# Choosing two experts batch by batch inside attention, with the gates computed beside the counting

## The reference

```python
logits = jnp.einsum('bsh,eh->bse', x, gate_w) + expert_bias
weights = jax.nn.softmax(logits, axis=-1)
top_w, top_i = jax.lax.top_k(weights, K)            # K = 2
top_w = top_w / (jnp.sum(top_w, axis=-1, keepdims=True) + GATE_EPS)
...                                                  # 8 experts, each token's two weighted and summed
out = (out - mu) * jax.lax.rsqrt(var + LN_EPS)
return out + x                                       # x here is the second layer norm's output
```

## Time and profile before

| | |
|---|---|
| three runs | 1274.6, 1275.29, 1277.65 us; median 1275.29 |
| the profiled execution | 1278.43 us, of which its span (first to last instruction) is 1276.7 us |
| busy share of the span | PE 87%, DVE 61%, POOL 65%, ACT 50% |
| attention, first to last `add_bias` | 77.7 to 715.0 us |
| tail of attention, from there to the first instruction of route | to 742.2 us |
| route | 742.2 to 793.6 us |
| experts | from 793.6 us |

### The profile page before, as it was taken

The page is one execution under the profiler, slowest core; times in us unless marked ns, Lnnn a source line. Parts: engine busy times, 40 slices in busy tenths (PEclk is TensorE's granted clock), DMA queues, the critical chain, the costliest instruction groups (busy, mean ns, idle before and its releaser), DMA issues. The chain is left out here.

```text
span 1276.7 us, 30578 instructions
## 1 busy us (share of the span) xinstructions
PE 1105.3 (87%) x11290; PEld 882.5 (69%) x11291; DVE 783.3 (61%) x2073; ACT 633.4 (50%) x904; POOL 832.1 (65%) x925
## 2 busy tenths in 40 slices
PE   5559999999999999999999717999999999999900
PEld 3237777777777777777777613888888888888800
DVE  4626668567576675766868566555555555555567
ACT  3438786776767777777777400222222222222222
POOL 2337587687776887768857521566766666666656
PEclk9769999999999999999999955999999999999955
DMA  8985854863558537565273182242434344432364
GB/s 281 289 213 130 245 146 115 202 142 99 139 141 190 140 100 161 141 139 170 61 180 101 69 281 66 39 113 48 115 49 108 47 111 112 90 74 45 45 163 135
DMA packets 122892, 167.14 MB, mean 131 GB/s; under 512 B 13048, under 2 KB 99320, under 8 KB 122784
## 3 DMA queue, kind: packets, MB, share of 16 engines
q1 hardware_dynamic: 103200, 137.59, 39.7%
q0 software_dynamic: 19584, 28.11, 11.9%
HBM read 105.22 MB, written 60.44 MB: 130 GB/s over the span
## 5 line engine op out<-in xcount | busy, mean ns | idle before, releaser
L983 DVE CUSTOM_DVE_ANT_0 b_sn<-b_ps_s,s_tile 128x512 f32<-128x512 f32 x512 | 341.5, 689 | 194.6 <-PE b_ps_s L1136 191.5
L920 ACT ACTIVATE b_pt<-b_ps_t 128x1024 f32<-128x1024 f32 x256 | 259.2, 1016 | 74.2 <-PE b_ps_t L1150 74.2
L1150 PE MATMUL b_ps_t<-ident,b_sn 128*128 128x128 f32 x2048 | 268.6, 274 | 3.1 <-POOL b_sn L820 2.0
L1150 PEld LDWEIGHTS b_ps_t<-ident,b_sn 128*128 128x128 f32 x2048 | 237.4, 141 | 41.0 <-issue 10.7
L1758 ACT ACTIVATE d_g<-d_ps_u 128x512 f32<-128x512 f32 x156 | 92.8, 598 | 305.8 <-PE d_ps_u L1871 216.5
L820 POOL TENSOR_SCALAR b_sn<-b_sn,b_mn 128x512 f32<-128x512 f32 x256 | 175.9, 698 | 97.8 <-DVE b_mn L983 97.4
L912 ACT ACTIVATE b_sn<-b_sn,b_mn 128x512 f32<-128x512 f32 x256 | 182.2, 723 | 94.6 <-DVE b_mn L983 87.5
L1136 PE MATMUL b_ps_s<-s_ks,s_qs 96*128 96x512 bf16 x512 | 179.2, 386 | 30.0 <-PEq L145 19.7
L1871 PE MATMUL d_ps_u<-d_xp,k_wu 128*128 128x256 bf16 x1776 | 201.5, 274 | 0.1
L1886 PE MATMUL d_ps_y<-k_wd,d_gp 128*128 128x256 bf16 x1776 | 199.9, 273 | 0.0
L1871 PEld LDWEIGHTS d_ps_u<-d_xp,k_wu 128*128 128x128 bf16 x1776 | 173.4, 98 | 21.9 <-issue 0.9
(11 more groups left out here) (237 smaller groups left out, 1171.4 us busy)
## 6 DMA issues: line engine op xcount, KB each, us to landing
w_parts<-b_w_split SPq DMA_DIRECT2D x32, 512.0 KB, 3.6
splits<-s_parts SPq DMA_DIRECT2D x32, 384.0 KB, 3.2
s_qs<-splits SPq DMA_DIRECT2D x96, 128.0 KB, 5.9
s_ks<-splits SPq DMA_DIRECT2D x96, 128.0 KB, 7.5
b_w_raw<-in_w_up_t SPq DMA_DIRECT2D x16, 512.0 KB, 11.1
b_w_raw<-in_w_down_t SPq DMA_DIRECT2D x16, 512.0 KB, 7.4
k_wu<-w_parts SPq DMA_DIRECT2D x8, 1024.0 KB
k_wd<-w_parts SPq DMA_DIRECT2D x8, 1024.0 KB
```

Of the source, the lines that this page charges most:

```text
L920: act.activation(pt[:, m, 2 * pair:2 * pair + 2, :], ps_t[:, 2 * pair:2 * pair + 2, :], ACT.Exp).then_inc(exped, 1)
L983: dve.tensor_tensor_reduce(sn[:, n % 2, t, :], ps_s[:, t % 2, :], ahead.tile[:, n, at:at + S], -1.0, BIG, ALU.add, ALU.min, mn[:, n % 2, t ...
L1150: mm = pe.transpose(ps_t[:, j, t * P:(t + 1) * P], sn[:, m, t, j * P:(j + 1) * P], ident[:, :])
```

## The change

1. `logits`, `top`, `top_i` and the two tiles that held the last rows (`xb`, `gated`) move into a class `Choice` that lives from attention to the end.
2. `keep_logits` adds the expert bias while it copies. The searches run on these biased logits and not on the softmax weights (the order is the same). For batch b - 2 they stand in batch b: four `max` at n = 1.5, two `max_index` at n = 2.5, two at n = 3.5. Batch 6's stand at the end of the last batch's heads, batch 7's behind the last logits.
3. In route the chain from the bias to the gates is gone from the DVE's beginning. After `both`, two subtractions (l - l1 for all eight, l2 - l1) are issued, ACT takes exp of both, and behind `kept.rows` the gates follow as 1 / (1 + e + eps * sum) and e times that.
4. In the tail of attention, the second half of the last rest moves from POOL to the DVE (two instructions, between the last copy for the logits and the logits). SP issues the last store of rest and no longer waits for it or for the rows there: route's SP waits ahead of the load of rest, route's POOL ahead of the first gathers.

```diff
@@ new class @@
+class Choice:
...
+        self.logits = sb("logits", [P, NT, NE])
+        self.e_bias = sb("e_bias", [P, NE])
+        self.top = sb("top", [P, NT, 8])
+        self.top_i = sb("top_i", [P, NT, 8], U32)
+        self.rows, self.rest = sb("rows", [P, TB, D]), sb("rest", [P, TB, D])
+        self.rows_out, self.rest_out = (ctx.enter_context(nc.semaphore("h_rows_out")),
+                                        ctx.enter_context(nc.semaphore("h_rest_out")))
@@ attention, SP @@
             by_batches(batch)
             store_h2(B - 1)
-            store_rest(B - 1)
-            sp.wait_ge(h2_out, 16 * B)
-            sp.wait_ge(rest_out, 16 * B)
+            sp.wait_ge(dve_end, by_dve("rest"))
+            sp.wait_ge(rest_done, B * 2 - 1)
+            sp.dma_start(rest_rows[B - 1, :, :].rearrange("(t p) d -> p t d", p=P), gated[:, :, :]).then_inc(rest_out, 16)
             sp.wait_ge(sums_zeroed, 16 * (B + 1))
             sp.wait_ge(w_stored, 16 * 4 * NE)
@@ attention, POOL @@
             deviation(B - 1)
-            for j in range(2):
-                rest_of(B - 1, j)
+            rest_of(B - 1, 0)
@@ attention, DVE @@
             def keep_logits(b, at):
                 dve.wait_ge(used, at + 1)
-                dve.tensor_copy(logits[:, bass.ds(b * TB, TB), :],
-                                ps_m[:, 0:TB * NE].rearrange("p (t e) -> p t e", e=NE)).then_inc(freed, 1)
+                dve.tensor_tensor(logits[:, b * TB:(b + 1) * TB, :], ps_m[:, 0:TB * NE].rearrange("p (t e) -> p t e", e=NE),
+                                  ahead.e_bias[:, :].unsqueeze(1).to_broadcast([P, TB, NE]), ALU.add).then_inc(freed, 1)
+
+            def largest(b):
+
+                for t in range(b * TB, (b + 1) * TB):
+                    dve.max(top[:, t, :], logits[:, t, :]).then_inc(topped, 1)
+
+            def largest_at(b, ts):
+
+                dve.wait_ge(topped, (b + 1) * TB)
+                apart(dve, dve_passed)
+                for t in ts:
+                    dve.max_index(top_i[:, b * TB + t, :], top[:, b * TB + t, :], logits[:, b * TB + t, :])
...
+                if b > 1:
+                    if n == 1.5:
+                        dve.wait_ge(freed, use(b - 1, "middle", "logits") + 1)
+                        apart(dve, dve_passed)
+                        largest(b - 2)
+                    if n == 2.5:
+                        largest_at(b - 2, (0, 1))
+                    if n == 3.5:
+                        largest_at(b - 2, (2, 3))
...
             by_batches(batch)
+            dve.wait_ge(freed, ALL_USES)
+            largest(B - 2)
+            largest_at(B - 2, range(TB))
             dve.wait_ge(pe_end, by_pe("turn0"))
...
+            mod = mod_last[:, 2 * D:3 * D].unsqueeze(1).to_broadcast([P, 2, D])
+            by_gate = ot[:, :].rearrange("p (t d) -> p t d", d=D)
+            dve.tensor_tensor(by_gate, xb[:, 2:4, :], mod, ALU.mult).then_inc(dve_end, 1)
+            dve.wait_ge(dve_end, by_dve("scaled"))
+            dve.tensor_tensor(gated[:, 2:4, :], gated[:, 2:4, :], by_gate, ALU.add).then_inc(dve_end, 1)
             dve.wait_ge(pe_end, by_pe("logits"))
-            dve.tensor_copy(logits[:, (B - 1) * TB:, :], ps_m[:, 0:TB * NE].rearrange("p (t e) -> p t e", e=NE))
+            dve.tensor_tensor(logits[:, (B - 1) * TB:, :], ps_m[:, 0:TB * NE].rearrange("p (t e) -> p t e", e=NE),
+                              ahead.e_bias[:, :].unsqueeze(1).to_broadcast([P, TB, NE]), ALU.add).then_inc(dve_end, 1)
+            dve.wait_ge(dve_end, by_dve("logits"))
+            largest(B - 1)
+            largest_at(B - 1, range(TB))
@@ route, SP @@
+            sp.wait_ge(choice.rest_out, 16 * B)
             sp.dma_start(kept.rest[:, :, :], rest_rows.rearrange("b (t p) d -> p (b t) d", p=P)).then_inc(kept_in, 16)
@@ route, POOL @@
             pool.wait_ge(tokens_set, 1)
+            pool.wait_ge(choice.rows_out, 16 * B)
@@ route, ACT @@
-            act.wait_ge(shifted, 1)
-            act.activation(weights[:, :, :], logits[:, :, :], ACT.Exp).then_inc(exped, 1)
+            act.wait_ge(shifted, 2)
+            act.activation(weights[:, :, :], weights[:, :, :], ACT.Exp).then_inc(exped, 1)
+            act.activation(per_tok[:, 1, :], per_tok[:, 0, :], ACT.Exp).then_inc(exped, 1)
@@ route, DVE @@
-            link(dve.tensor_tensor(logits[:, :, :], logits[:, :, :], e_bias[:, :].unsqueeze(1).to_broadcast([P, NT, NE]), ALU.add))
-            link(dve.tensor_reduce(per_tok[:, 0, :], logits[:, :, :], AX.X, ALU.max))
...
-            for t in range(NT):
-                ins = dve.max(top[:, t, :], weights[:, t, :])
-            link(ins)
-            for t in range(NT):
-                ins = dve.max_index(top_i[:, t, :], top[:, t, :], weights[:, t, :])
-            link(ins)
-            link(dve.tensor_tensor(per_tok[:, 3, :], top[:, :, 0], top[:, :, 1], ALU.add))
...
             link(dve.tensor_copy(top_f[:, :, :], top_i[:, :, 0:2]))
             dve.wait_ge(consts_ready, 9)
...
             dve.tensor_tensor(both[:, :, :], hot[:, 0, :, :], hot[:, 1, :, :], ALU.add).then_inc(hot_done, 1)
+
+
+            dve.tensor_tensor(weights[:, :, :], logits[:, :, :], top[:, :, 0:1].to_broadcast([P, NT, NE]), ALU.subtract).then_inc(shifted, 1)
+            dve.tensor_tensor(per_tok[:, 0, :], top[:, :, 1], top[:, :, 0], ALU.subtract).then_inc(shifted, 1)
 
             dve.wait_ge(ranked, 1)
...
             link(dve.tensor_copy(kept.rows[:, :, :], places[:, :, :]))
+            dve.wait_ge(exped, 2)
+            link(dve.tensor_reduce(per_tok[:, 2, :], weights[:, :, :], AX.X, ALU.add))
+            link(dve.scalar_tensor_tensor(out=per_tok[:, 2, :], in0=per_tok[:, 2, :], scalar=GATE_EPS, in1=per_tok[:, 1, :],
+                                          op0=ALU.mult, op1=ALU.add))
+            link(dve.tensor_scalar(per_tok[:, 2, :], per_tok[:, 2, :], 1.0, None, ALU.add))
+            link(dve.reciprocal(per_tok[:, 3, :], per_tok[:, 2, :]))
+            dve.tensor_copy(kept.gates[:, 0, :], per_tok[:, 3, :]).then_inc(gates_set, 1)
+            dve.tensor_tensor(kept.gates[:, 1, :], per_tok[:, 3, :], per_tok[:, 1, :], ALU.mult).then_inc(gates_set, 1)
             rows = kept.rows[:, :, :].rearrange("p k t -> p (k t)")
```

More of the change, by code:

```diff
@@ L56, in make_identity, with __init__, sb @@
                        pattern=[[-1, P]], channel_multiplier=1).then_inc(done, 1)
+class Choice:
+    def __init__(self, nc, ctx):
+        def sb(name, shape, dt=F32):
+            return ctx.enter_context(nc.sbuf_tensor("h_" + name, shape, dt))
+        self.logits = sb("logits", [P, NT, NE])
[5 more added lines that the diff above has]
+                                        ctx.enter_context(nc.semaphore("h_rest_out")))
 class Ahead:
@@ L498, with attention @@
 FROM_BEFORE = ("back3", "turn0", "turn1", "out0", "out1", "rows0", "rows1", "logits")
-def attention(nc, ahead, logits, x, h1t, mod_rows, ext_rows, splits, w_up_t, w_down_t, w_parts, rest_rows, h2_rows, sums):
+def attention(nc, ahead, choice, x, h1t, mod_rows, ext_rows, splits, w_up_t, w_down_t, w_parts, rest_rows, h2_rows, sums):
     GROUPS = NH // TB
@@ L528, in attention @@
         ont = sb("ont", [P, DC, S])
-        xb = sb("xb", [P, TB, D])
+        logits, top, top_i, xb, gated = choice.logits, choice.top, choice.top_i, choice.rows, choice.rest
         ga = sb("ga", [P, D])
         gab = sb("gab", [P, D])
-        gated = sb("gated", [P, TB, D])
         mod2 = sb("mod2", [P, 3 * D])
@@ L583, in attention @@
                    "rows00", "rows01", "rows10", "rows11", "logits")
-        DVE_ENDS = ("ont0", "on", "ont1b", "rows0", "rows1")
+        DVE_ENDS = ("ont0", "on", "ont1b", "rows0", "rows1", "scaled", "rest", "logits")
         def by_pe(name):
@@ L1350, in __init__, with route @@
         self.wd = sb("wd", [P, 2, PIECES, NIC, D], BF16)
-def route(nc, kept, logits, rest_rows, mod_rows, e_bias, w_parts, gate_rows, h2_rows):
+def route(nc, kept, choice, rest_rows, mod_rows, w_parts, gate_rows, h2_rows):
     FILLS = TABLE * TT
@@ L1477, in _ @@
             link(dve.memset(swing[:, 1:NE:2], -1.0))
-            link(dve.tensor_tensor(logits[:, :, :], logits[:, :, :], e_bias[:, :].unsqueeze(1).to_broadcast([P, NT, NE]), ALU.add))
-            link(dve.tensor_reduce(per_tok[:, 0, :], logits[:, :, :], AX.X, ALU.max))
-            dve.tensor_tensor(logits[:, :, :], logits[:, :, :], per_tok[:, 0, :].unsqueeze(2).to_broadcast([P, NT, NE]),
-                              ALU.subtract).then_inc(shifted, 1)
-            dve.wait_ge(exped, 1)
-            link(dve.tensor_reduce(per_tok[:, 1, :], weights[:, :, :], AX.X, ALU.add))
-            link(dve.reciprocal(per_tok[:, 2, :], per_tok[:, 1, :]))
-            link(dve.tensor_tensor(weights[:, :, :], weights[:, :, :], per_tok[:, 2, :].unsqueeze(2).to_broadcast([P, NT, NE]), ALU.mult))
-            for t in range(NT):
-                ins = dve.max(top[:, t, :], weights[:, t, :])
-            link(ins)
-            for t in range(NT):
```

(7 more changed lines are left out.)

20 lines of the change are left out of this document (9 added, 11 removed).

## The result

The changed kernel took a median of 1266.07 us over five runs (1263.28 to 1269.97), the kernel before 1274.6 over five runs (1271.43 to 1277.65), the three from which the forecast started among them. The ratio is 0.9945, 95% interval 0.9924 to 0.9966: faster by 4.3 to 9.7 us, and the forecast of 7.6 lies inside. The median of 1266.07 lies inside the stated 1264.5 to 1271.5.

A forecast was written before the change was run, and what follows sets the result against it. One serial stretch from attention's end through route to experts, in which steps hang mostly on the DVE, was taken as the bound. 3.1 + 6.1 - 0 - 1.55 - 0 = 7.6 us less than 1275.29 gives 1267.7; range 1264.5 to 1271.5.

The forecast's parts named there:

- The end of attention: From the last logits to route's start: without POOL's second half and SP's wait, route starts 3.1 us earlier (2.9 to 3.25).
- The tail: DVE work behind the last logits: bias and copy, four maxima, four index searches, together 1.26 us.
- the meeting point: Between attention's last engine and route's start: taken as 0.35 us, between bounds of 0.2 and 0.5.
- Rest on the DVE: Two added DVE passes before the last logits, 0.69 to 1.33 us each, hidden behind PE's logits.
- The start of route: DVE chain to `hot`, 11.43 us before: now POOL's constants are late, `hot` comes after 5.35, gain 6.1 us.
- The subtractions: Between `both` and the ranks in route: 0.42 and 0.21 us fit the DVE's idle 0.70, cost 0 (0 to 0.1).
- The gates: In route, between `kept.rows` and the places' bits: on the path in full, a loss of 1.55 us (1.4 to 1.9).
- The slots: Searches in attention's batches 2 to 7: hidden where the DVE waits for PE, cost 0; without cover 6.2 us.
- The first: Rival at attention's end: the store is waited for all the same, gain 5.9 us, time 1269.4; chance 0.12.
- second: Rival in attention: the searches there are on the path, 6.2 of 7.6 us go, time 1273.9; chance 0.06.
- third: Rival in attention: index searches cost far more there, at 2 us per slot the time is 1284; chance 0.02.
- The fourth: Rival in route's token search: PE returns to full clock, 5 us more gain, time 1263; chance 0.04.

## Why the prediction was right

**The end of attention** was worth 3.05 against 3.1, by two errors of opposite sign. The tail took 1.39 and not 1.26 (the maxima start 0.04 behind the copy's end, but the first index search only 0.15 behind the maxima's), and the meeting point 0.26 and not 0.35. That the sum fits to 0.05 is partly luck. The two bounds, 0.2 and 0.5, belonged to different last engines. The DVE's drain here ends at 731.4, 0.04 behind its last search, and route begins 0.2 behind it; with POOL computing both halves route begins 0.2 behind SP's drain too, but that drain stands 0.3 behind the end of SP's issue. So the 0.35 lay between two cases and belonged to neither.

**Rest on the DVE.** The two passes took 2.35 us together, from 727.03 to 729.38, within 1.38 and 2.66, and 0.61 of PE's logits remained as cover. The split differs from what was worked out: the DVE's first pass began 0.05 ahead of POOL's addition and took its plain 0.68; POOL's took 1.75 instead of 1.27; the DVE's second pass took 1.64 and ended 0.55 behind POOL's end at 728.83, so it too got hardly anything done until then. The Trainium skill (SBUF — State Buffer, Who interferes with whom) has whoever issues second wait for the whole of the first; the trace agrees to within 0.15, with the DVE first this time: by the rule POOL would end at 727.71 + 1.27 = 728.98 and the second pass at 728.83 + 0.68 = 729.51. The sum was the same by both, as stated.

**The start of route.** `hot` came 5.33 behind route's first instruction, forecast 5.35, released by the constant that was named. Two small errors cancel in it: POOL took 5.22 for its constants and not 5.30, and the DVE followed 0.11 behind the last one and not 0.05. The step was right, but it also names what the change leaves on the table: of the 11.43 that the DVE had there, 5.33 stay because of nine signals where `hot` needs two. The experiment with the constants in order shows 4.63 of them gone, 3.63 of it at experts.

**The subtractions** fitted: the idle time ahead of the copy fell from 0.70 to 0.24, and the copy comes 1.92 behind `hot` as before. **The gates** cost 1.48 (forecast 1.55), and moving them behind the feed returned 1.47. **The slots** cost nothing: idle 0.63 became 0.35 behind the four maxima, and even three times the work left the batch at 81.8.

**The rivals.** The first is refuted by SP's drain of 7 ns and by the 1.17 that the explicit wait costs. The second and third would need longer batches; at six times the work the cost is 0.3 per batch and 1.06 in the last one. The fourth is refuted by the clock of 0.50. Its price rested on a wrong reading: the DVE is not busy through all of the search, its feed ends at 777.66 in the trace of before and PE goes on alone for 7.21 us.

The terms' bounds add up to 8.25 at the upper end and not to 8.1, which changes nothing here. The forecast for the median, 1267.7, is 1.6 above what was measured. That is within the spread of the runs: it subtracted from a median of 1275.29, with two more runs that median is 1274.6, and with the later kernels the kernel before had medians of 1273.2 to 1274.1 over nine to eleven runs and 1276.98 in a single one.

## What to carry to other kernels

When work is taken from the front of a stage, price the gain up to what is late next, not by the work removed: 6.8 us of searches moved away brought 0.9, since constants built on another engine were due at 5.3 anyway. With the constants in order of need, where `hot` comes at 0.70, the same move would be worth some 5.5 (an estimate, 7.43 - 0.70 less the tail's 1.18; that pair was not run). One wait for all constants is a wait for the slowest; ordering them by need and splitting the wait brought 3.6 more. And when a stage moves forward in time, look at what now runs beside it: a DVE chain pulled onto POOL's long instructions lost 1.0 to 1.5 us that no wait in the profile showed, only durations three to six times too long.

## What the runs showed of the hardware

- A DVE instruction and a POOL instruction on SBUF can exclude each other, and it depends on the kind. An addition with two SBUF inputs took 1.23 instead of 0.35 beside POOL's cast, and 0.34 again when the cast stood on ACT. The subtraction with two SBUF inputs in that last version (738.70) kept its 0.42 beside the 1.40 us iota, which reads nothing. A plain f32 copy took 1.03 instead of 0.18 beside such an iota; the addition right behind that copy took 0.94, and whether it was held itself or only queued behind the copy is not shown. The Trainium skill, on the page and section named above, says both: two-input instructions contend with GpSimd instructions that read SBUF and not with those that only write it, and copies can enter a two-port mode, in which they contend with GpSimd. The runs here fit both halves, by the 0.42 and the 1.03; that these copies ran in such a mode is not shown.
- A drain of SP lasts 7 ns with a store in flight. POOL's at the end of attention ends at 729.4, 0.5 behind its last addition (728.83); its drain before experts lasts 7.2 us and ends 2.0 behind the last gather's issue (775.28 + 0.95). What it waits for behind the gathers was not tried.
- The next block begins 0.2 behind the end of the last drain, whether that is the DVE's (731.4), POOL's (778.3) or SP's (736.7 with POOL computing both halves). A DVE that is last reaches the end of its drain 0.04 behind its work, an SP that is last 0.3 behind its issue, which makes 0.26 and 0.51 in all.
